# A mixture-of-experts stage in a sequence-and-expert kernel: experts written out, rows found two experts at a time, four gathered ahead

## The reference: what is computed

```
h = attention within a segment, q = k = v = x (softmax of x x^T / 16)
h = h + selective_scan_block(layernorm(h))        # state 16, inner width 512, conv of 4 taps
h = h + experts(layernorm(h))                     # 64 experts, 8 for each token
```

```
pos = cumsum(one_hot(e)) - 1 of the token's own expert;  valid = pos < CAP
buf[e, pos] = x[token]
y = (silu(buf @ w_gate) * (buf @ w_up)) @ w_down
out[token] += y[e, pos] * topk_w * valid
```

## Time and profile before

| | |
|---|---|
| three runs | 3309.37, 3311.04 (median), 3313.46 us |
| profiled execution | 3304.55 us, span 3302.7 us |
| mean granted TensorE clock | 0.959 |
| PE busy over the span | 2943.3 us (89%) |
| DVE busy | 2808.4 us (85%) |
| ACT busy | 2730.5 us (83%) |
| POOL busy | 2259.9 us (68%) |
| expert stage | from about 2840 us to the end, about 463 us |

### The profile page before, as it was taken

How to read it: one execution, slowest core, us unless ns; L and a number is a source line. 1 busy time by engine, 2 the same in 40 slices (tenths; PEclk the granted TensorE clock), 3 DMA queues, 4 the chain that set the end, 5 groups by cost and what they waited for, 6 DMA issues and landing times. The chain is left out here.

```text
span 3302.7 us, 55009 instructions
## 1 busy us (share of the span) xinstructions
PE 2943.3 (89%) x18817; PEld 2370.4 (72%) x18817; DVE 2808.4 (85%) x4597; ACT 2730.5 (83%) x5297; POOL 2259.9 (68%) x940
## 2 busy tenths in 40 slices
PE   6999999999999999999999999999999986665664
PEld 4777777777777777777777777777777775544543
DVE  4899999999999999999999999999999997344432
ACT  5999999999999999999999999999999995211110
POOL 1777777677777777676767777776767774377776
PEclk8999999999999999999999999999999998688887
DMA  3112222122222222121112222222222121477774
GB/s 111 58 59 68 70 70 70 58 64 64 70 70 70 70 70 70 61 70 64 62 59 69 70 70 70 70 70 70 70 70 70 51 65 30 118 145 152 148 150 75
DMA packets 196160, 252.80 MB, mean 77 GB/s; under 512 B 45664, under 2 KB 174144, under 8 KB 195904
## 3 DMA queue, kind: packets, MB, share of 16 engines
q1 hardware_dynamic: 171328, 211.73, 20.4%
q0 software_dynamic: 24576, 37.77, 6.9%
HBM read 188.36 MB, written 61.08 MB: 76 GB/s over the span
## 5 line engine op out<-in xcount | busy, mean ns | idle before, releaser
L345 POOL TENSOR_TENSOR hid<-hid,c_all 128x1536 f32<-128x1536 f32 x512 | 1768.4, 3460 | 842.2 <-DVEq L607 821.0
L612 DVE TENSOR_TENSOR_SCAN hid<-decay,hid,psB 128x1024 f32<-128x1024 f32 x512 | 1201.5, 2347 | 82.8 <-PE psB L914 35.2
L386 ACT ACTIVATE decay<-dt,a_neg 128x383 f32<-128x383 f32 x2048 | 1085.8, 604 | 0.5 <-issue 0.2
L914 PE MATMUL psB<-ident,dbu_t 128*128 128x128 f32 x6144 | 852.2, 275 | 87.9 <-DVE hid L612 61.8
L374 ACT ACTIVATE dbu_t<-dtu_t,b_t 128x512 f32<-128x512 f32 x1376 | 893.2, 710 | 4.1 <-PE psB L914 4.0
L914 PEld LDWEIGHTS psB<-ident,dbu_t 128*128 128x128 f32 x6144 | 700.0, 141 | 200.2 <-issue 87.1
L926 PE MATMUL psY<-ident,hid 128*128 128x128 f32 x6144 | 754.3, 273 | 0.1
L926 PEld LDWEIGHTS psY<-ident,hid 128*128 128x128 f32 x6144 | 687.2, 141 | 0.6 <-POOL hid L345 0.4
L612 DVE TENSOR_TENSOR_SCAN hid<-decay,psB 128x512 f32<-128x512 f32 x512 | 623.7, 1218 | 9.6 <-PE psB L914 5.2
L996 PE MATMUL psM<-u,w_dt 128*128 128x384 f32 x1024 | 351.5, 487 | 3.8 <-ACT u L416 3.1
L1407 ACT ACTIVATE e_side<-e_psL,e_in_tile 128x128 f32<-128x128 f32 x128 | 45.8, 363 | 261.9 <-DVE e_in_tile L1531 261.2
(11 more groups left out here) (148 smaller groups left out, 3260.6 us busy)
## 6 DMA issues: line engine op xcount, KB each, us to landing
c_all<-bc_rows_dram SPq DMA_DIRECT2D x128, 768.0 KB, 5.0
out_dram<-h SPq DMA_DIRECT2D x64, 384.0 KB, 5.7
h<-out_dram SPq DMA_DIRECT2D x32, 384.0 KB, 3.5
x_weights_dram<-normed SPq DMA_DIRECT2D x32, 384.0 KB, 2.6
xt<-in_x_t_dram SPq DMA_DIRECT2D x32, 375.0 KB
xs<-in_x_dram SPq DMA_DIRECT2D x32, 256.0 KB
e_wg<-in_gate_dram SPq DMA_DIRECT2D x64, 128.0 KB, 2.8
e_wu<-in_up_dram SPq DMA_DIRECT2D x64, 128.0 KB, 3.0
```

Of the source, the lines that this page charges most:

```text
L345: nc.gpsimd.tensor_tensor(hid[k % 4][:, :, :], hid[k % 4][:, :, :], c_all[:, k, :].unsqueeze(1).to_broadcast([P, CH, L]), ALU.mult).then_i ...
L386: last = nc.scalar.activation(decay[k % 4][:, c, 1:L], dt[q][:, c, 1:L], ACT.Exp, scale=a_neg[:, c, k:k + 1])
L612: nc.vector.tensor_tensor_scan(h[:, lo:hi], flat(decay[k % 4])[:, lo:hi], flat(psB)[:, lo:hi], h[:, lo - 1:lo] if j else 0.0, ALU.mult, AL ...
L914: last = nc.tensor.transpose(flat(psB)[:, i * P:(i + 1) * P], dbu_t[k % 2][:, t, c * P:(c + 1) * P], ident[:, :])
```

## The change

Only `expert_phase` changes; the operations on the data of an expert stay the same.

- All 64 experts are written out on every engine, with constants in place of registers; the loop, its branches and the `s_turn` increments that carried waits go away.
- Rows are found in rounds of two experts (PAIR = 2) instead of eight: 32 calls of `find_rows` instead of 8, on tiles of 4 columns instead of 16.
- Six experts instead of 16 are located before the first is computed, and after that expert e + 6 is located beside expert e.
- Indices are handed out two experts at a time, at even e for e + 4 and e + 5, instead of one at a time six ahead.
- POOL gathers four experts, and then for each e first scatters e and then gathers e + 4.
- PE runs one expert ahead instead of two: for each e `turn(e+1)`, `gather_counts(e+6)`, `down(e)`, `up(e+1)`. DVE accordingly copies the turned rows of e + 1.

On PE, from `turn(3)` on, before: `e_psG` is written by `turn`, `e_psL` by `gather_counts`, `e_psO` by `down`, `e_psU` by `up`.

The diff:

```diff
     AHEAD = 4
-    STAGED = 6
-    NR = NE // EB
-    LOCATED = 2
+    LOCATED = 6
+    PAIR = 2
     FIN = 5
     R = NT + 1
     UW = P + 2
-    W = EB * NH
+    W = PAIR * NH
     I = w["gate"].shape[2]
...
-        def each(eng, body):
-
-            for q in range(EB):
-                body(0, q, q)
-            with eng.Fori(1, NR - LOCATED) as i:
-                for q in range(EB):
-                    body(i, EB * i + q, q)
-            for i in range(NR - LOCATED, NR):
-                for q in range(EB):
-                    body(i, EB * i + q, q)
-
-        def exists(e):
-            return not isinstance(e, int) or e < NE
-
-        def to_locate(e, q):
-
-            return e + LOCATED * EB, q % 2
-
         @block.sync
         def _(sp):
 
             sp.wait_ge(s_z, 1)
             sp.dma_start(h_out[NTOK:NTOK + CAP, :].rearrange("(h p) d -> p h d", p=P), zero[:, :, :]).then_inc(s_zst, 16)
 
-            def load(e, q):
+            for e in range(NE):
+                q = e % EB
+                after(sp, s_yo, e - EB + 1)
...
-            for q in range(EB):
-                load(q, q)
-            with sp.Fori(1, NE // EB) as i:
-                for q in range(EB):
-                    sp.wait_ge(s_yo, EB * i + q - EB + 1)
-                    sp.sem_inc(s_turn, 1)
-                    load(EB * i + q, q)
...
-            def gather(e, q):
+            def gather(e):
+                q = e % EB
                 pool.wait_ge(s_st, e + 1)
-                pool.sem_inc(s_turn, 1)
                 for h in range(NH):
...
-            def scatter(e, q):
+            def scatter(e):
                 pool.wait_ge(s_ys, e + 1)
                 after(pool, s_sc, 16 * NH * e)
-                pool.sem_inc(s_turn, 1)
                 for h in range(NH):
...
-                gather(e, e)
+                gather(e)
             pool.wait_ge(s_zst, 16)
-
-            def expert(i, e, q):
-                if exists(e + AHEAD):
-                    gather(e + AHEAD, (q + AHEAD) % EB)
-                scatter(e, q)
-
-            each(pool, expert)
+            for e in range(NE):
+                scatter(e)
+                if e + AHEAD < NE:
+                    gather(e + AHEAD)
...
-            def expert(i, e, q):
-                if exists(e + 1):
-                    silu(e + 1, (q + 1) % EB)
-                if exists(to_locate(e, q)[0]):
-                    count(*to_locate(e, q))
-
-            for e in range(LOCATED * EB):
-                count(e, e % 2)
-            silu(0, 0)
-            each(act, expert)
+            for e in range(LOCATED):
+                count(e)
+            silu(0)
+            for e in range(NE):
+                if e + 1 < NE:
+                    silu(e + 1)
+                if e + LOCATED < NE:
+                    count(e + LOCATED)
...
-            def turn(i, e, q):
-                r = q % 2
-                pe.wait_ge(s_xg[q], 16 * NH * (i + 1))
+            def turn(e):
+                q, r = e % EB, e % 2
+                pe.wait_ge(s_xg[q], 16 * NH * (e // EB + 1))
...
-            def expert(i, e, q):
-                if exists(e + 1):
-                    up(i + (q + 1) // EB, e + 1, (q + 1) % EB)
-                if exists(e + 2):
-                    turn(i + (q + 2) // EB, e + 2, (q + 2) % EB)
-                if exists(to_locate(e, q)[0]):
-                    gather_counts(*to_locate(e, q))
-                down(i, e, q)
...
-            for e in range(LOCATED * EB):
-                gather_counts(e, e % 2)
-            turn(0, 0, 0)
-            up(0, 0, 0)
-            turn(0, 1, 1)
-            each(pe, expert)
+            for e in range(LOCATED):
+                gather_counts(e)
+            turn(0)
+            up(0)
+            for e in range(NE):
+                if e + 1 < NE:
+                    turn(e + 1)
+                if e + LOCATED < NE:
+                    gather_counts(e + LOCATED)
+                down(e)
+                if e + 1 < NE:
+                    up(e + 1)
...
-            def stage(e, q):
-                nc.vector.tensor_copy(src_st[q][:, :], src[:, bass.ds(e * NH, NH)])
-                nc.vector.tensor_copy(dst_st[q][:, :], dst[:, bass.ds(e * NH, NH)]).then_inc(s_st, 1)
-
-            def copy_turned(e, q):
-                r = q % 2
+            def stage(e):
+                q = e % EB
+                after(dve, s_sc, 16 * NH * (e - EB + 1))
+                nc.vector.tensor_copy(src_st[q][:, :], src[:, e * NH:(e + 1) * NH])
+                nc.vector.tensor_copy(dst_st[q][:, :], dst[:, e * NH:(e + 1) * NH]).then_inc(s_st, 1)
...
-            def expert(i, e, q):
-                r = q % 2
+            def activate(e):
+                q, r = e % EB, e % 2
                 dve.wait_ge(s_sg, e + 1)
                 nc.vector.tensor_tensor(at[r][:, :], sg[r][:, :], psU[r][:, 1, :], ALU.mult).then_inc(s_at, 1)
-                nc.vector.tensor_copy(wcol[r][:, :], xg[q][:, :, bass.ds(D + e, 1)].rearrange("p h o -> p (h o)")
-                                      ).then_inc(s_wc, 1)
-                if exists(to_locate(e, q)[0]):
-                    pass_tiles(*to_locate(e, q))
-                if exists(e + 2):
-                    copy_turned(e + 2, (q + 2) % EB)
+                nc.vector.tensor_copy(wcol[r][:, :], xg[q][:, :, D + e]).then_inc(s_wc, 1)
...
-                if q == 1 and (not isinstance(i, int) or 0 < i < NR - 1):
-                    find_rows(i + 1)
-                if exists(e + STAGED):
-                    after(dve, s_sc, 16 * NH * (e + STAGED - EB + 1))
-                    stage(e + STAGED, (q + STAGED) % EB)
-                if exists(to_locate(e, q)[0]):
-                    enter_tiles(*to_locate(e, q))
...
-                dve.wait_ge(s_pl, EB * (r + 1))
-                part = lambda t: t[:, bass.ds(r * W, W)]
+                dve.wait_ge(s_pl, PAIR * (r + 1))
+                part = lambda t: t[:, r * W:(r + 1) * W]
                 by_expert = lambda t: t.rearrange("p (e h) -> p e h", h=NH)
...
-            pass_tiles(0, 0)
-            for e in range(LOCATED * EB):
-                if e + 1 < LOCATED * EB:
-                    pass_tiles(e + 1, (e + 1) % 2)
-                enter_tiles(e, e % 2)
-                if e % EB == EB - 1:
-                    find_rows(e // EB)
-                if e == EB - 1:
-                    for j in range(STAGED):
-                        stage(j, j)
-            copy_turned(0, 0)
-            copy_turned(1, 1)
-            each(dve, expert)
+            pass_tiles(0)
+            for e in range(LOCATED):
+                if e + 1 < LOCATED:
+                    pass_tiles(e + 1)
+                enter_tiles(e)
+                if e % PAIR == 1:
+                    find_rows(e // PAIR)
+                    for j in (e - 1, e):
+                        if j < AHEAD:
+                            stage(j)
+            copy_turned(0)
+            for e in range(NE):
+                activate(e)
+                if e + LOCATED < NE:
+                    pass_tiles(e + LOCATED)
+                if e + 1 < NE:
+                    copy_turned(e + 1)
+                scale(e)
+                if e % PAIR == 0 and e + AHEAD < NE:
+                    if e > 0:
+                        find_rows((e + AHEAD) // PAIR)
+                    for j in range(e + AHEAD, e + AHEAD + PAIR):
+                        stage(j)
+                if e + LOCATED < NE:
+                    enter_tiles(e + LOCATED)
```

49 lines of the change are left out of this document (27 added, 22 removed).

## The result

The changed kernel took 3290.22 us (median of 9 runs, 3281.56 to 3299.53), the kernel before 3309.37 (9 runs, 3302.68 to 3313.46): ratio 0.9946 [0.993, 0.9962]. It is faster by 0.5%. In the sessions further down, executions in a slower state of the chip, of which there were a few, are left out of every ratio and mean. The forecast was 3306 with the range 3298 to 3319. The profiled execution took 3281.56 us (span 3279.5, mean granted clock 0.965), 23 us less than that of before.

What follows compares the result with a forecast made beforehand. The prediction took a chain of scatters in the expert stage to bound the kernel; start -7.0, loop -1.3 and code +3.6 summed to -4.7 us on the median 3311.04, so 3306, range 3298 to 3319.

Steps and rivals of the forecast that it cites:

- What bounds the kernel: Expert stage: a chain of scatters and their landing, gathers in its shadow, about 6.6 us per expert; no engine full.
- The steady state at 0: Middle of the expert stage: POOL's and PE's reorderings shift alike, so the scatter chain keeps its period; 0 us.
- their cover: Expert stage: scaled rows ready 8 us before their scatter, a spare that hides 24 added find_rows calls on DVE.
- The start, -7.0: Start of the expert stage: rounds of two and shorter PE queue bring the first scatter earlier; -7.0 us.
- The loop (-1.3): Loop experts of the stage: removing register arithmetic and branches saves at most 0.033 us on each of 40; -1.3 us.
- the code (+3.6): Expert stage written out: 11 more instruction packets, some delaying a scatter's landing; +3.6 us, bounds 0 and 13.
- The price of 0.33 us per packet: Expert stage: mean delay per code packet, from 2.6 us of long waits ahead of three scatters.
- The slower rival: Written-out code costs what it did in the first eight experts, 0.58 us each above the loop; 3326 us, 12%.
- The faster rival: Packets miss the landings and the first eight experts' excess goes; -12.7 us, 3298 us, 12%.

Runs made afterwards that it cites:

- after_two_ahead: Changed kernel with PE and DVE two experts ahead again, scatter still ahead of gather; ratio to the kernel before 1.0 [0.9988, 1.0012], +1.5 ± 1.7 us.
- before_again: The kernel before run and profiled once more, nothing changed; ratio to the kernel before 1.0004 [0.999, 1.0018].
- after_looped: Changed kernel with experts 8 to 55 in a loop of six turns on every engine; ratio to the kernel before 0.9945, and 0.9946 when repeated.
- before_one_ahead: Kernel before with PE and DVE only one expert ahead, POOL's order kept; ratio to the kernel before 1.0084 [1.0065, 1.0103], +27 ± 2.3 us.
- before_one_ahead_late_loads: before_one_ahead with expert e's weight load also waiting until the scatter of expert e - 10 has landed; ratio to the kernel before 0.9981 [0.9965, 0.9996].

## Why the prediction was wrong

The sum was -4.7 us; the stage gave, over the profiles of both, about -9.5 (461.2, mean of two, against 451.7, mean of four).

**What bounds the kernel** held: the chain of scatters, with the same period and the same gap in both. **The steady state at 0** held too, and after_two_ahead shows what it hung on. DVE's added find_rows calls stayed in their cover: scaled rows are ready 7.5 us ahead of their scatter (median; at the least 5.0), where the prediction had 8. The 10.4 us that POOL's row gives to DVE's scaled rows are the first scatter's 6.74 and seven ordinary gaps.

**The start, -7.0: right in mechanism, undersized.** On the profiled pair the terms were: copy_turned(0) 6.18 us earlier (forecast 5.8; from the start of find_rows to the gather it took 1.66 us with 4 columns, not 2.37), from copy to activation 5.04 instead of 5.43, activation to `down(0)` 1.00 instead of 2.59 (forecast 0.8), and 3.31 instead of 2.89 from there to the scatter, since `down(0)` ran for 1.53 us instead of 1.08, at a mean granted clock of 0.71. Together -7.74. But before's start was read from one profile, 30.29, near the low end of a quantity that ranges from 30.1 to 32.9: copy_turned(0) stands there behind a second find_rows of eight experts, at +19.4 to +21.4. The changed kernel has no such spread. The mean gain is 8.9.

**The loop (-1.3) and the code (+3.6): the failed step, as far as the profiles show it.** Together they were +2.3, and the rest of the stage measured 429.2 against 429.9, nothing that can be told from 0. The price of 0.33 us per packet came from three long waits in one trace, and none of them came back in before_again, with the same packets; over ten profiles the difference is 0.23 for a 16 KB packet and 0.08 for one of 8 KB, and 8 of the 13 added packets are the small ones. The step that failed is this price, taken as that of every packet. Whether the term itself was too large stays open, since the timed comparisons of written out against looped give +4.8 ± 1.4 us where the profiles of the changed kernel's stage give nothing. The Trainium skill (Runtime: NRT & Kernel Launch, Instruction fetch mechanics) has a taken branch stall when its target is not among the fetched pages. No run here shows such a cost: after_looped is at least as fast as the written-out kernel.

**The first eight experts.** The slower rival rested wholly on their 57.34 us as a property of the code. One more profile of the same program gave 53.65. The faster rival took the same excess as something the change removes, which was no better founded.

**The level and the range.** With the start at -8.9 and the rest at 0, the forecast would have been 3302, inside the range. Of the 12 us from there to 3290.2, 1.7 are the level of before (3311.04 over three runs, 3309.37 over nine), and about 6 lie between the first session's gain, 17.5 us, and the 11.7 of the three later ones. What is left of the 12 is the 2.8 between that 11.7 and the start's 8.9, and 1.6 between medians and means. So the two terms that were mis-sized account for about 4 us of a miss of 16; of the rest no stage of the profiles shows the place. The range counted the unknown costs of the change, but not that stage start and rest of one program differ by 17 and 6 us between executions, so that medians of a few runs differ by several us. It was too narrow at the lower end.

**What stays open.** 11.7 ± 1.1 us timed against 9.5 in the stage's profiles: with two and four profiles the 2 us can be chance. The gap is wider for the looped version: some 17 us timed, 9.4 in its stage's two profiles, 8.5 of them at the start. And if writing out costs what the timed runs say, the other parts of the change gain more than the start accounts for. That the sequence phase falls into quicker executions more often with the change is not borne out by the starts of the stage in the 18 profiles, whose means agree within 0.3 us, but these are too few to exclude a few us. Where the difference lies is not known.

## What to carry to other kernels

Where a chain of dependent transfers sets the period, ask of each reordering only when the first link starts and what other transfers meet its landing; work that lies in the cover, as 24 more calls of find_rows here, need not cost anything. Before a term is taken from a stretch of one profile (57.34 us, a start of 30.29, three long waits), look for how far the same quantity varies between stretches that should be alike, and put that into the range. And undo the halves of a double reordering one at a time. Here each came out dearer than both together: the old order in the changed kernel by 2.5 us at the first scatter, the old depth by 4.2 there and some 10 in the rest of the stage, and the new depth in the kernel before by 27 us, the last by moving the weight loads and not by the wait one would look for.

## What the runs showed of the hardware

- The same set of weight loads (384 KB) costs nothing that can be told when it leaves on the median 4.4 to 5.8 us after the start of a pair of accumulating scatters, and 0.6 us per period when it leaves at 2.7, with the same DMA work in all: 288.12 us against 263.55 for 40 experts. It is the place against the landing that costs, not the bytes: without any loads it is 262.43.
- Periods of the scatters in which a 16 KB or an 8 KB code packet started were 0.23 and 0.08 us longer on the mean, sorted over ten profiles. Going from 25 to 37 packets in the stage showed no cost (450.34 us, +1.4 ± 2.6); for the step from 11 or 12 to 24 or 25 the profiles of the changed kernel's stage show none and the timed runs 4.8 ± 1.4 us.
- 28 transposes with waits between them left PE at a granted clock of 0.50 up to and over the first product of the first expert.
- The part of the program ahead of the stage is identical in all kernels, and yet the stage began anywhere in 17 us: POOL's MEMSET in the earliest and the latest profile, before_one_ahead and before_one_ahead_late_loads.

```profile
2830.08 0.20 POOL L1360 MEMSET e_ident<- 128x128 f32 x1 [28.31 <-POOLq L1149]
```

```profile
2847.37 0.21 POOL L1359 MEMSET e_ident<- 128x128 f32 x1 [28.19 <-POOLq L1149]
```

Half a per cent of the whole kernel comes and goes there without any change to it, as much as the change gained.
